# Attention step on TensorE: transposes of the probabilities issued behind the value matmuls of the step instead of ahead of them

## The chip, the cores and the metric

The kernel runs on one core of one Trainium2 chip. The metric is the device time of one launch in microseconds (us). Three runs of the kernel before took 2483.66, 2484.05 and 2486.16 us; the median is 2484.05. A traced execution of it is the source of all profile rows below.

Engines go by the names of the profile: PE is the matrix engine (PEld its weight loads), DVE the vector engine, ACT the scalar engine, POOL the GpSimd engine, SP the engine that issues transfers.

## The reference

Input x is 4 x 1024 tokens of 256 features. One layer in "macaron" form:

```python
x = x + 0.5 * ffn(layernorm(x))       # 8 experts, top 2, and a shared one
x = x + attn(layernorm(x))
x = x + 0.5 * ffn(layernorm(x))
```

The part that matters here is the attention, with 16 heads of 64 features and all 1024 x 1024 scores of each head and batch:

```python
q, k, v = (_ln(x, s, b) @ W + bias for each of q, k, v)
scores = einsum('bhqd,bhkd->bhqk', q, k) / 16
mask = triu(full((S, S), -999.0), k=S - 1)
p = softmax(scores + mask, axis=-1)
att = einsum('bhqk,bhkd->bhqd', p, v)
```

The mask touches one element of each 1024 x 1024 table, the last key of the first query. All of it is in float32. The kernel splits operands into a high and a low part in the matrix engine's reduced float32 format, so that a product is two or three matmuls.

## The kernel before

Four phases follow each other, each written as one function per engine: a feed-forward phase (tiles f_...), the attention (a_...), the output projection and the layer's own MLP (m_...), and the second feed-forward phase (g_...). Engines are kept in step by semaphores that are waited for and counted; the order of instructions on each engine is that of the code.

The attention works in **steps**. A step handles one tile of 128 queries of one head: 64 head-and-batch pairs x 8 tiles = 512 steps. They are grouped in 16 **iterations** of 32 steps (k = 0 to 31; two pairs of heads of one batch), of which 14 run in a hardware loop. Behind them comes a short last part that empties the pipeline. What is computed for one tile is spread over several steps:

- In step k, PE computes the scores of the tile (line 1493, four matmuls of 512 columns into `sc`, which has two buffers). DVE takes the negated row maximum (line 1410), ACT the exponential with its row sum (line 1262, into `pr`).
- In step k + 1, DVE takes the reciprocal of the sum (line 1415) and POOL scales the row (line 1335, `normed`).
- In step k + 3 (`LAG = 3`), PE transposes the 128 x 1024 probabilities with eight transposes in two halves (line 1505, into `tr`, one buffer of two banks, one per half). ACT copies each half to the high part of `pT` (line 1256, `tr_hi`), DVE subtracts it from `tr` and so writes the low part (line 1421, `tr_lo`). `pT` has two buffers, each for four tiles, i.e. 512 queries.
- When four tiles are there they form a **block**. There are 128 of them. The values of a block (line 1529) are 16 matmuls of 512 columns that accumulate in the one bank `ov`. They are cut into four parts of four matmuls, one per step, q = 0 to 3. A block starts (q = 0) in the steps k = 3, 7, 11, ... 31, one step behind the transposes of its last tile. When its last part is done, ACT reads one half of `ov`'s partitions with the bias (line 1249, `ov_read`) and DVE copies the other half (line 1401, `half`). The next block's first matmul waits for both.
- In 12 of the 32 steps PE also computes one piece of the projections of the heads to come (`piece_at`, lines 1448 and 1457, into `pj`): in k = 1, 3, 5, 9, 17, 19, 21, 23, 25, 27, 29 and 31. ACT stages it, POOL splits it.

The order in a step on each engine is this. PE: scores, transposes, values, piece. ACT: read of `ov` if a block has ended in the step before, the two copies of the transposes, the exponential, the staging of the piece. DVE: copy of `ov` if a block has ended, maximum, reciprocal for the step before, the two low parts. POOL: scaling for the step before, the addition of the two head halves at every fourth block, the pieces.

The waits of PE in a step are these: the scores wait for the exponential two steps back (it frees `sc`). The transposes wait for `normed`, and each half of them for the low part of the same half of the tile before (it frees `tr`). At q = 0 the values wait for `tr_lo` of the tile transposed in the step before, for `ov_read` and for `half`:

```python
if q == 0:
    pe.wait_ge(s["tr_lo"], 2 * (u - LAG))
    ...
    if not (first and blk == 0):
        pe.wait_ge(s["ov_read"], it * BLOCKS + blk)
        pe.wait_ge(s["half"], it * BLOCKS + blk)
```

SP moves the second pair's values from a side buffer at the start of each iteration (line 1114), doubles the keys (line 1110), loads weights and stores results.

Of the kernel before, what the change touches and what calls it, by code (L numbers as in the profile page):

```python
# [27 lines left out]
P = 128  # L28
# [916 lines left out]
def attention_phase(nc, turns, tag, w, zT, w_split, bias, att):  # L945
# [14 lines left out]
    LAG = 3  # L960
    QT = S // P
    NP = 4
# [470 lines left out]
    def on_tensor(pe, ahead):  # L1433
# [36 lines left out]
        def body(it, first, last):  # L1470
            for k in steps(last):
                u = it * ITER + k
                slot, head, tile = k // STEPS, (k // QT) % 2, k % QT
                if not last:

                    if k % STEPS == 0:

                        pe.wait_ge(s["k_dup"], it * 64 + slot * 32 + 32)
                        if slot:
                            pe.wait_ge(s["split"], before(it, STEPS))  # L1480
                        elif not first:
                            pe.wait_ge(s["split"], before(it, 0) - 3)
                        else:
                            pe.wait_ge(s["first_split"], 3)
                            pe.wait_ge(f["res"], NB * 2)
                    if first and k == 4:
                        pe.wait_ge(s["first_split"], 4)
                    if not (first and k < 2):

                        pe.wait_ge(s["exp"], u - 1)  # L1490
                    for kb in range(S // BT):
                        for a in range(2):
                            o = pe.matmul(sc[:, k % 2, kb * BT:(kb + 1) * BT],  # L1493
                                          q_s[:, slot, head, tile * P:(tile + 1) * P],
                                          k_s[:, slot, head, a, kb * BT:(kb + 1) * BT],
                                          start=(a == 0), stop=(a == 1))
                    o.then_inc(s["sc"], 1)
                if transposes_at(k, first, last):
                    pe.wait_ge(s["normed"], u - LAG + 1)
                    for part in range(2):  # L1500
                        if not (first and k == LAG):

                            pe.wait_ge(s["tr_lo"], 2 * (u - LAG) + part - 1)
                        for j in range(4):
                            o = pe.transpose(tr[:, part, j * P:(j + 1) * P],  # L1505
                                             pr[:, (k - LAG) % NP, (4 * part + j) * P:(4 * part + j + 1) * P], ident[:])
                        o.then_inc(s["tr"], 1)
                v = values_at(k, first)
                if v and not (last and v[2] >= 0):
                    vslot, vhead, blk, q = v  # L1510
                    if q == 0:

                        pe.wait_ge(s["tr_lo"], 2 * (u - LAG))
                        if blk == 0 and first:
                            pe.wait_ge(s["split"], before(it, 4))
                            pe.wait_ge(f["zT_lo"], (NB + 1) * DC)
                        elif blk == 0:

                            pe.wait_ge(s["split"], before(it, 0))
                        if blk == 4:  # L1520

                            pe.wait_ge(s["v_in"], it * 16 + 16)
# [4 lines that stand above are left out]
                    for kt in (2 * q, 2 * q + 1):  # L1527
                        for a in range(2):
                            o = pe.matmul(ov[:], v_s[:, vslot, kt, 2 * vhead:2 * vhead + 2]  # L1529
                                          .rearrange("p k f -> p (k f)"), pT[:, blk % 2, a, kt],  # L1530
                                          start=(kt == 0 and a == 0), stop=(kt == QT - 1 and a == 1))
                    if q == 3:
                        o.then_inc(s["pv"], 1)
                if not last and piece_at(it, k):
                    kind, part, n, _ = piece_at(it, k)
                    if kind == "K" and part == 0:
                        pe.wait_ge(s["wqk_in"], it * 64 + (k // STEPS) * 32 + 64)
                        if k >= STEPS:
                            pe.wait_ge(s["z_in"], it * 32 + 64)
                    if kind == "V" and part == 0:  # L1540
                        pe.wait_ge(s["wv_in"], it * 16 + 32)
                    project(kind, part, n, False)
                if ends(it) and k == STEPS + 4:
                    ahead["b1"](pj)
                if first and k in (5, 6):
                    if k == 6:
                        pe.wait_ge(f["zT_lo"], NB * DC + 1)
                    rest["zT_up"](k - 5, ov[:])
# [512 lines left out]
```

## Time and profile before

| what | value |
|---|---|
| median of three runs | 2484.05 us |
| profiled execution, its own time | 2480.43 us |
| its span | 2478.6 us |
| PE busy | 2415.1 us, 97% |
| PEld busy | 2097.6 us, 85% |
| DVE busy | 1893.6 us, 76% |
| ACT busy | 1664.7 us, 67% |
| POOL busy | 1505.0 us, 61% |
| granted clock, mean | 0.996 |

The span is what the trace covers, and 1.8 us of the profiled execution's time lie around it. Busy time is that of an engine's instructions; weight loads are counted apart, since they overlap matmuls. The ends of matmuls are modelled, so that a row's duration says less than the distance from its start to the start of the next. A row of the timeline merges neighbouring instructions of the same kind ("x4") and gives in brackets how long the engine had been idle before and who ended that. [...]

### The profile page before, as it was taken

How to read it: one execution, taken by the hardware profiler on the slowest of the kernel's cores; microseconds unless marked ns; L12 is line 12 of the kernel's file. 1: busy time of each engine (PE TensorE's matmuls, PEld its weight loads, DVE VectorE, ACT ScalarE, POOL GpSimd, SP SyncE). 2: the span in 40 equal slices, each digit the busy share in tenths (PEclk: the TensorE clock that was granted, in tenths of full speed). 3: DMA queues.
4: the chain of work that ended last, by engine and by line, in shares of the span. 5: the costliest groups of instructions: out<-in, count | busy, mean ns of one | idle time of the engine just before them, and what ended most of it. 6: DMA issues, size and time to landing. Idle time of an engine off the chain costs nothing.

```text
span 2478.6 us, 46572 instructions
## 1 busy us (share of the span) xinstructions
PE 2415.1 (97%) x14544; PEld 2097.6 (85%) x14544; DVE 1893.6 (76%) x3626; ACT 1664.7 (67%) x2879; POOL 1505.0 (61%) x1525
## 2 busy tenths in 40 slices
PE   7999979999999999999999999999999999989999
PEld 7888868888888888888888888888888879988888
DVE  4777667878888787887878878788887877766665
ACT  2455567878787787877878778787777853433333
POOL 1233277777776878777787777777768754342211
PEclk9999999999999999999999999999999999999999
DMA  3522432213222122321213212132221354431111
GB/s 134 230 102 87 168 99 73 94 43 98 72 76 94 43 85 72 89 94 43 85 60 93 89 47 93 43 97 72 76 94 43 113 178 152 138 104 35 51 51 43
DMA packets 128038, 220.15 MB, mean 89 GB/s; under 512 B 6922, under 2 KB 89764, under 8 KB 119076
## 3 DMA queue, kind: packets, MB, share of 16 engines
q1 hardware_dynamic: 127908, 218.78, 27.4%
q8 instruction: 37, 0.61, 0.1%
q14 instruction: 93, 0.76, 0.1%
HBM read 114.95 MB, written 53.48 MB: 68 GB/s over the span
## 4 chain that ended last, share of the span: by engine, by line
PE 81%; DVE 8%; issue 6%; POOL 2%; ACT 2%; DMA 1%; SPq 0%; DVEq 0%; ACTq 0%; POOLq 0%
PE a_ov L1529 19%; PE a_sc L1493 18%; PE a_tr L1505 18%; PE a_pj L1448 7%; PE a_pj L1457 4%; PE g_acc L856 3%; PE g_hid L819 3%; PE f_hid L819 2%; PE f_acc L856 2%; PE m_proj L1920 1%; PE f_gbc L898 1%; PE m_acc L1957 1%; DVE f_hp L656 1%; PE m_hid L1986 1%; DVE g_hp L656 1%
## 5 line engine op out<-in xcount | busy, mean ns | idle before, releaser
L1410 DVE TENSOR_REDUCE a_nmax<-a_sc 128x1 f32<-128x1024 f32 x512 | 626.6, 1224 | 259.3 <-PE a_sc L1493 251.0
L1335 POOL TENSOR_SCALAR a_pr<-a_pr,a_rden 128x1024 f32<-128x1024 f32 x512 | 578.1, 1130 | 257.5 <-DVE a_rden L1415 186.5
L1256 ACT ACTIVATE a_pT<-a_tr 128x512 fp32r<-128x512 f32 x1024 | 560.1, 596 | 208.7 <-PE a_tr L1505 202.7
L1421 DVE TENSOR_TENSOR a_pT<-a_tr,a_pT 128x512 fp32r<-128x512 f32 x1024 | 649.4, 676 | 17.5 <-ACT a_pT L1256 17.5
L1529 PE MATMUL a_ov<-a_pT,a_v_s 128*128 128x512 f32 x2048 | 600.5, 415 | 3.2 <-DVE a_half L1401 2.0
L1262 ACT ACTIVATE a_pr<-a_sc,a_nmax 128x1024 f32<-128x1024 f32 x512 | 574.0, 1121 | 32.6 <-DVE a_nmax L1410 29.5
L1493 PE MATMUL a_sc<-a_k_s,a_q_s 128*128 128x512 f32 x2048 | 555.5, 393 | 7.8 <-DMA a_k_s<-a_k_s 7.5
L1505 PEld LDWEIGHTS a_tr<-f_ident,a_pr 128*128 128x128 f32 x4096 | 473.8, 140 | 92.2 <-DVE a_pT L1421 18.5
L1505 PE MATMUL a_tr<-f_ident,a_pr 128*128 128x128 f32 x4096 | 537.6, 273 | 9.2 <-DVE a_pT L1421 9.1
L1493 PEld LDWEIGHTS a_sc<-a_k_s,a_q_s 128*128 128x128 f32 x2048 | 381.0, 189 | 89.0 <-DMA a_k_s<-a_k_s 7.7
L1529 PEld LDWEIGHTS a_ov<-a_pT,a_v_s 128*128 128x128 f32 x2048 | 347.5, 189 | 54.4 <-issue 5.0
L1448 PE MATMUL a_pj<-a_z_s,a_wqk_s 128*128 128x512 f32 x756 | 193.5, 391 | 0.6 <-issue 0.6
L1448 PEld LDWEIGHTS a_pj<-a_z_s,a_wqk_s 128*128 128x128 f32 x756 | 141.7, 188 | 32.7 <-issue 1.0
L454 ACT ACTIVATE g_act_out<-g_hid,f_b 128x512 f32<-128x512 f32 x72 | 49.6, 689 | 148.7 <-PE g_hid L819 148.7
L1225 ACT ACTIVATE a_staged<-a_pj,f_bias 128x512 f32<-128x512 f32 x126 | 86.9, 689 | 88.5 <-PE a_pj L1448 66.3
L454 ACT ACTIVATE f_act_out<-f_hid,f_b 128x512 f32<-128x512 f32 x72 | 49.3, 685 | 119.0 <-PE f_hid L819 119.0
L856 PEld LDWEIGHTS f_acc<-f_w2p,f_hp 128*128 128x128 f32 x864 | 112.1, 190 | 9.3 <-DVE f_hp L656 4.5
L856 PEld LDWEIGHTS g_acc<-g_w2p,g_hp 128*128 128x128 f32 x864 | 112.1, 190 | 8.2 <-DVE g_hp L656 2.9
L856 PE MATMUL f_acc<-f_w2p,f_hp 128*128 128x256 f32 x864 | 115.9, 284 | 2.4 <-DVE f_hp L656 1.8
L856 PE MATMUL g_acc<-g_w2p,g_hp 128*128 128x256 f32 x864 | 115.5, 283 | 1.3 <-DVE g_hp L656 0.9
L819 PE MATMUL f_hid<-f_xT,f_w1p 128*128 128x512 f32 x432 | 115.9, 405 | 0.0
L819 PE MATMUL g_hid<-g_xT,g_w1p 128*128 128x512 f32 x432 | 113.1, 397 | 0.0
(207 smaller groups left out, 3281.7 us busy)
## 6 DMA issues: line engine op xcount, KB each, us to landing
a_z_s<-zT SPq DMA_DIRECT2D x32, 1024.0 KB, 7.7
a_k_s<-a_k_s SPq DMA_DIRECT2D x64, 512.0 KB, 5.6
a_wqk_s<-w_split SPq DMA_DIRECT2D x64, 256.0 KB, 3.1
a_v_s<-a_v_b SPq DMA_DIRECT2D x16, 1024.0 KB, 4.6
att<-a_ao SPq DMA_DIRECT2D x32, 512.0 KB, 2.9
m_in<-att SPq DMA_DIRECT2D x16, 1024.0 KB, 6.0
a_wv_s<-w_split SPq DMA_DIRECT2D x17, 512.0 KB, 3.8
zT<-f_zT SPq DMA_DIRECT2D x8, 1024.0 KB, 3.9
```

The lines of the kernel that those rows point to most:

```text
L819: o = pe.matmul(hid[:, (par + e) % 2], w1p[:, a, (c * NE + x) * HID:(c * NE + x + 1) * HID], xT[:, par, c, b], start=(n == 0), stop=(n == 5))
L856: o = pe.matmul(acc[:, t], hp[:, e % 3, a, t * P:(t + 1) * P], w2p[:, b, x * D:(x + 1) * D], start=False, stop=(e == NE - 1 and (a, b) == ...
L1256: act.activation(pT[:, (u // 4) % 2, 0, 4 * part:4 * part + 4, (u % 4) * P:(u % 4 + 1) * P], tr[:, part].rearrange("p (t q) -> p t q", t=4 ...
L1262: act.activation(pr[:, k % NP], sc[:, k % 2], ACT.Exp, bias=nmax[:, k % NP:k % NP + 1], accum_out=den[:, k % NP:k % NP + 1]).then_inc(s["e ...
L1335: pool.tensor_scalar(pr[:, k % NP], pr[:, k % NP], rden[:, k % NP:k % NP + 1], 1.0, ALU.mult, ALU.mult).then_inc(s["normed"], 1)
L1410: dve.tensor_reduce(nmax[:, k % NP:k % NP + 1], sc[:, k % 2], AX.X, ALU.max, negate=True).then_inc(s["negmax"], 1)
L1421: dve.tensor_tensor(to[:, 1], tr[:, part].rearrange("p (t q) -> p t q", t=4), to[:, 0].bitcast(F32), ALU.subtract).then_inc(s["tr_lo"], 1)
L1448: o = pe.matmul(bank[:], wqk_s[:, "QK".index(kind), c, a], z_s[:, c * 2 + b, part], start=(i == 0), stop=(i == 5))
L1457: o = pe.matmul(bank[:, t * 2 * P:(t + 1) * 2 * P], z_s[:, c * 2 + a, part // 2, col:col + P], wv_s[:, c, b], start=(i == 0), stop=(i == 5))
L1493: o = pe.matmul(sc[:, k % 2, kb * BT:(kb + 1) * BT], q_s[:, slot, head, tile * P:(tile + 1) * P], k_s[:, slot, head, a, kb * BT:(kb + 1) * ...
L1505: o = pe.transpose(tr[:, part, j * P:(j + 1) * P], pr[:, (k - LAG) % NP, (4 * part + j) * P:(4 * part + j + 1) * P], ident[:])
L1529: o = pe.matmul(ov[:], v_s[:, vslot, kt, 2 * vhead:2 * vhead + 2] .rearrange("p k f -> p (k f)"), pT[:, blk % 2, a, kt], start=(kt == 0 an ...
```

## The change

The block of code that issues the transposes is moved, within the step on PE, from ahead of the value matmuls to behind them. It stays ahead of the projection piece. Waits and counts are the same. Nothing in the functions of the other engines changes.

```diff
                     o.then_inc(s["sc"], 1)
-                if transposes_at(k, first, last):
-                    pe.wait_ge(s["normed"], u - LAG + 1)
-                    for part in range(2):
-                        if not (first and k == LAG):
-
-                            pe.wait_ge(s["tr_lo"], 2 * (u - LAG) + part - 1)
-                        for j in range(4):
-                            o = pe.transpose(tr[:, part, j * P:(j + 1) * P],
-                                             pr[:, (k - LAG) % NP, (4 * part + j) * P:(4 * part + j + 1) * P], ident[:])
-                        o.then_inc(s["tr"], 1)
                 v = values_at(k, first)
                 if v and not (last and v[2] >= 0):
...
                     if q == 3:
                         o.then_inc(s["pv"], 1)
+                if transposes_at(k, first, last):
+                    pe.wait_ge(s["normed"], u - LAG + 1)
+                    for part in range(2):
+                        if not (first and k == LAG):
+
+                            pe.wait_ge(s["tr_lo"], 2 * (u - LAG) + part - 1)
+                        for j in range(4):
+                            o = pe.transpose(tr[:, part, j * P:(j + 1) * P],
+                                             pr[:, (k - LAG) % NP, (4 * part + j) * P:(4 * part + j + 1) * P], ident[:])
+                        o.then_inc(s["tr"], 1)
                 if not last and piece_at(it, k):
```

The order on PE before, at the turn from one block to the next in a step without a piece: the last part of a block's values (the first row), the next step's scores and transposes, and the first part of the next block's values, with its waits.

```order
L1529 MATMUL a_ov<-a_pT,a_v_s 128x512 x4
L1493 MATMUL a_sc<-a_k_s,a_q_s 128x512 [waits a_exp]
L1493 MATMUL a_sc<-a_k_s,a_q_s 128x512 x3
L1505 MATMUL a_tr<-f_ident,a_pr 128x128 [waits a_tr_lo,a_normed]
L1505 MATMUL a_tr<-f_ident,a_pr 128x128 x3
L1505 MATMUL a_tr<-f_ident,a_pr 128x128 [waits a_tr_lo]
L1505 MATMUL a_tr<-f_ident,a_pr 128x128 x3
L1529 MATMUL a_ov<-a_pT,a_v_s 128x512 [waits a_half,a_ov_read,a_tr_lo]
L1529 MATMUL a_ov<-a_pT,a_v_s 128x512 x3
```

The same place with the change (the values are now line 1519, the transposes line 1531):

```order
L1519 MATMUL a_ov<-a_pT,a_v_s 128x512 x4
L1531 MATMUL a_tr<-f_ident,a_pr 128x128 [waits a_tr_lo,a_normed]
L1531 MATMUL a_tr<-f_ident,a_pr 128x128 x3
L1531 MATMUL a_tr<-f_ident,a_pr 128x128 [waits a_tr_lo]
L1531 MATMUL a_tr<-f_ident,a_pr 128x128 x3
L1493 MATMUL a_sc<-a_k_s,a_q_s 128x512 [waits a_exp]
L1493 MATMUL a_sc<-a_k_s,a_q_s 128x512 x3
L1519 MATMUL a_ov<-a_pT,a_v_s 128x512 [waits a_half,a_ov_read,a_tr_lo]
L1519 MATMUL a_ov<-a_pT,a_v_s 128x512 x3
```

The transposes between the last part of a block and the first part of the next are now those of the earlier step; those of the later step come behind the waiting row.

A step with a projection piece on PE, before, from the transposes on:

```order
L1505 MATMUL a_tr<-f_ident,a_pr 128x128 [waits a_tr_lo,a_normed]
L1505 MATMUL a_tr<-f_ident,a_pr 128x128 x3
L1505 MATMUL a_tr<-f_ident,a_pr 128x128 [waits a_tr_lo]
L1505 MATMUL a_tr<-f_ident,a_pr 128x128 x3
L1529 MATMUL a_ov<-a_pT,a_v_s 128x512 x4
L1448 MATMUL a_pj<-a_z_s,a_wqk_s 128x512 [waits a_staged,a_z_in,a_wqk_in]
L1448 MATMUL a_pj<-a_z_s,a_wqk_s 128x512 x5
```

The same step with the change:

```order
L1519 MATMUL a_ov<-a_pT,a_v_s 128x512 x4
L1531 MATMUL a_tr<-f_ident,a_pr 128x128 [waits a_tr_lo,a_normed]
L1531 MATMUL a_tr<-f_ident,a_pr 128x128 x3
L1531 MATMUL a_tr<-f_ident,a_pr 128x128 [waits a_tr_lo]
L1531 MATMUL a_tr<-f_ident,a_pr 128x128 x3
L1448 MATMUL a_pj<-a_z_s,a_wqk_s 128x512 [waits a_staged,a_z_in,a_wqk_in]
L1448 MATMUL a_pj<-a_z_s,a_wqk_s 128x512 x5
```

The piece stays last in its step; it now follows the transposes directly. DVE, ACT, POOL and SP have the same rows in the same order before and after.

## Rows read from the trace of the kernel before

**Rows 1.** The page: the span, and PE's busy time and share.

```profile
span 2478.6 us, 46572 instructions
...
PE 2415.1 (97%) x14544; PEld 2097.6 (85%) x14544; DVE 1893.6 (76%) x3626; ACT 1664.7 (67%) x2879; POOL 1505.0 (61%) x1525
```

**Rows 2.** The page: the chain that ended last, by engine and by line.

```profile
PE 81%; DVE 8%; issue 6%; POOL 2%; ACT 2%; DMA 1%; SPq 0%; DVEq 0%; ACTq 0%; POOLq 0%
PE a_ov L1529 19%; PE a_sc L1493 18%; PE a_tr L1505 18%; PE a_pj L1448 7%; PE a_pj L1457 4%; PE g_acc L856 3%; PE g_hid L819 3%; PE f_hid L819 2%; PE f_acc L856 2%; PE m_proj L1920 1%; PE f_gbc L898 1%; PE m_acc L1957 1%; DVE f_hp L656 1%; PE m_hid L1986 1%; DVE g_hp L656 1%
```

**Rows 3.** Stretches: length, busy us per engine, granted clock, DMA share, GB/s.

```profile
346.00:2001.00 1655.00, 1647.32 (x9550) 1401.42 (x9551) 1345.59 (x2211) 1317.80 (x2329) 1259.45 (x1285) 1.00 0.25 77
```

**Rows 4.** Timeline of PE, 1198 to 1216 us: start, length, engine, line, tile.

```profile
1198.70 1.54 PE L1448 MATMUL a_pj<-a_z_s,a_wqk_s 128*128 128x512 f32 x6
1200.08 1.07 PE L1493 MATMUL a_sc<-a_k_s,a_q_s 128*128 128x512 f32 x4
...
1211.10 1.08 PE L1493 MATMUL a_sc<-a_k_s,a_q_s 128*128 128x512 f32 x4
1212.01 1.04 PE L1505 MATMUL a_tr<-f_ident,a_pr 128*128 128x128 f32 x8
1212.81 1.17 PE L1529 MATMUL a_ov<-a_pT,a_v_s 128*128 128x512 f32 x4
1213.82 1.08 PE L1493 MATMUL a_sc<-a_k_s,a_q_s 128*128 128x512 f32 x4
1214.74 1.03 PE L1505 MATMUL a_tr<-f_ident,a_pr 128*128 128x128 f32 x8
1215.56 1.17 PE L1529 MATMUL a_ov<-a_pT,a_v_s 128*128 128x512 f32 x4
```

**Rows 5.** Timeline of ACT and then of DVE, 1212 to 1216 us.

```profile
1212.65 1.09 ACT L1256 ACTIVATE a_pT<-a_tr 128x512 fp32r<-128x512 f32 x2 [0.53 <-PE a_tr L1505]
1213.62 1.12 ACT L1262 ACTIVATE a_pr<-a_sc,a_nmax 128x1024 f32<-128x1024 f32 x1
...
1214.71 0.68 ACT L1249 ACTIVATE a_ao<-a_ov,f_bias 64x512 f32<-64x512 f32 x1
...
1212.21 1.22 DVE L1410 TENSOR_REDUCE a_nmax<-a_sc 128x1 f32<-128x1024 f32 x1 [0.23 <-PE a_sc L1493]
...
1213.42 1.27 DVE L1421 TENSOR_TENSOR a_pT<-a_tr,a_pT 128x512 fp32r<-128x512 f32 x2
1214.72 0.69 DVE L1401 COPY a_half<-a_ov 64x512 f32<-64x512 f32 x1
```

**Rows 6.** The instructions of line 1401: count, ns of one, first and last start.

```profile
L1401 DVE COPY a_half<-a_ov x128: 683/688/694, 358.9 to 2014.7; 64x512 f32<-64x512 f32 x128
```

**Rows 7.** Timeline of PE, ACT and DVE at the attention's end, 2005 to 2015 us.

```profile
2005.05 1.16 PE L1505 MATMUL a_tr<-f_ident,a_pr 128*128 128x128 f32 x8 [0.73 <-DVE a_pT L1421]
...
2009.14 5.50 PE L1529 MATMUL a_ov<-a_pT,a_v_s 128*128 128x512 f32 x16 [2.00 <-DVE a_half L1401]
...
2014.47 0.40 PE L1920 MATMUL m_proj<-m_wo,m_att_hi 128*128 128x256 f32 x2
...
2006.35 1.10 ACT L1256 ACTIVATE a_pT<-a_tr 128x512 fp32r<-128x512 f32 x2
...
2006.99 1.29 DVE L1421 TENSOR_TENSOR a_pT<-a_tr,a_pT 128x512 fp32r<-128x512 f32 x2 [1.49 <-ACT a_pT L1256]
2008.31 0.68 DVE L1401 COPY a_half<-a_ov 64x512 f32<-64x512 f32 x1
```

**Rows 8.** Timeline of SP: the value move of the second and of the fifteenth iteration.

```profile
452.61 0.51 SPq L1114 DMA_DIRECT2D a_v_s<-a_v_b  x1
...
1822.45 0.52 SPq L1114 DMA_DIRECT2D a_v_s<-a_v_b  x1
```

**Rows 9.** Stretches (columns as in rows 3) with the granted clock.

```profile
330.00:346.00 16.00, 11.01 (x62) 7.90 (x62) 11.66 (x24) 13.24 (x26) 12.10 (x18) 1.00 0.36 127
...
2010.00:2012.00 2.00, 2.00 (x6) 1.61 (x5) 2.00 (x2) 0.00 (x0) 0.00 (x0) 0.50 0.00 0
```

## The prediction, made before the change was run

> **What bounds the kernel now.** I read the page's busy shares first. PE is busy 97% of the 2478.6 us span [rows 1], and the chain of waits gives PE 81% of it, more than half of the span to three lines of the attention step: 1529 (values, ov), 1493 (scores, sc) and 1505 (transposes, tr) [rows 2]. The table of stretches then says where: from 346 to 2001 us PE is busy 1647 of 1655 us at full clock, DVE 1346, ACT 1318, POOL 1259 [rows 3]. So attention is bound by PE's own instructions, and anything that makes PE stand still there goes into the time in full.
>
> The timeline of PE gives a step's pace, start to start: sc to tr 0.91 (1211.10 to 1212.01), tr to ov 0.80, ov to sc 1.01 [rows 4], together 2.72 us. A projection piece adds 1.38 (pj to sc) [rows 4]. An iteration of the loop has 32 steps and 12 pieces, so 32 x 2.72 + 12 x 1.38 = 103.6 us if PE never waits. The trace has 13 iterations between two issues of the value move, 1822.45 - 452.61 = 1369.8 us, 105.4 each [rows 8]. PE thus waits only 1.8 us per iteration now, some 29 us over the 16.
>
> What matters is why PE hardly waits at the turn of a block. The values of one block take four steps (q = 0 to 3) and accumulate in the one PSUM bank ov. At q = 0 PE must wait until the last block's ov was read by ACT (line 1249) and DVE (line 1401), and until the transposes of the step before are copied (tr_lo). The trace shows such a turn: ACT's read runs from 1214.71 to 1215.39, DVE's copy from 1214.72 to 1215.41 [rows 5], and ov starts at 1215.56 [rows 4]. That ov came only 0.82 after the transposes ahead of it instead of 0.80. The reads started at 1214.71, just as PE went into the new step's transposes (1214.74), and these 0.8 us of transposes are exactly what covers them.
>
> **The change, part by part.** Nothing is added or removed: PE has the same instructions with the same waits, and DVE, ACT, POOL and SP the same work in the same order. PE's order in a step becomes sc, ov, tr, piece.
>
> 1. Pace without waits. Before, the handovers in a step were 512 columns to 128 (sc to tr), 128 to 512 (tr to ov), 512 to 512 (ov to sc or pj). After, they are 512 to 512 (sc to ov), 512 to 128 (ov to tr), 128 to 512 (tr to sc or pj): the same kinds once each. I take zero. As a bound, a group of four 512-column matmuls takes 0.91 or 1.01 depending on its neighbours [rows 4]; if one group of each step changed between these, 512 steps would give 51 us either way.
>
> 2. The turn of a block. Call T the start of the last transposes ahead of the turn (step q = 3). Until now PE ran tr, then ov (q = 3), sc and tr of the next step, then ov (q = 0): from T that is 0.80 + 1.01 + 0.91 + 0.80 = 3.52 us of work. Now it runs only tr and sc: T + 0.80 + 1.01 = T + 1.81. (I take tr to sc as the 0.80 of tr to ov and sc to ov as the 1.01 of ov to sc.) What must be done by then stands in fixed order on the two other engines:
> ACT: first half of pT 0.64 after the transposes start (1212.01 to 1212.65), the exponential 0.97 later (1213.62), the read of ov 1.09 later (1214.71), 0.68 long [rows 4, 5], and 0.17 from its end (1215.39) to ov's start (1215.56). Sum 0.64 + 0.97 + 1.09 + 0.68 + 0.17 = 3.55 us.
> DVE: pT's low part 0.64 after ACT's first copy starts (2006.35 to 2006.99), 1.32 to the copy of ov (2008.31), 0.68 long, and 0.15 to ov [rows 7]; with the same 0.64 ahead that is 3.43.
> That 3.55 just meets 3.52 is why the turn costs nothing today. In the new order ov stands at T + 1.81 and has to wait until T + 3.55: 1.74 us of standstill, and behind the waiting ov all of PE's queue stands too, this step's transposes, the piece and the next scores. None of the work can fill the gap: no piece lies in a step with q = 3 (pieces are at 1, 3, 5, 9, 17, 19, 21, 23, 25, 27, 29, 31; q = 3 at 2, 6, 10, and so on). Is the exponential late for another reason? It needs the maximum of its step. The transposes of the step before start at T - 2.72, so DVE ends their low part at T - 2.72 + 0.64 + 0.64 + 1.30 = T - 0.14, and the maximum (1.21 from start to the next work [rows 5]) at T + 1.07, while ACT comes to the exponential at T + 1.61. So no. Nor does DVE become the bound: 4 x (1.21 + 1.30) + 0.7 = 10.7 us in a block that will last 4 x 2.72 + 1.74 = 12.6.
> There are 128 blocks [rows 6]. One has no block before it and the last turn lies behind the last scores, where the trace already shows this very wait (2.00 us idle, put down to the copy of ov [rows 7]); it stays. That leaves 126 turns: 126 x 1.74 = 219 us.
>
> 3. Waits that go. The 29 us worked out above are waits of the transposes for DVE and small ones at turns. In the new order the transposes come 1.0 later than the scores, so DVE has that much longer, and the turn's gap takes in the rest. I let them all go: -29. The bound on the other side is 0.
>
> 4. Last iteration and DMA. Without scores and with three transposes left, the order is set by waits on DVE's copies both times: zero. Key, query, weight loads and the att stores hang on pieces and blocks, which all come later together: zero.
>
> Sum: 219 - 29 = +190 us. The profiled execution took 2480.4 and would become 2670; the median of the runs is 2484.05, 3.6 above it, and would be **2674 us**.
>
> [...]
> [...]
>
> **The rivals.**
> A. The clock falls at the turns. For it: the tail. Price: the 16 value matmuls behind the standstill took 2009.14 to 2014.47 = 5.33 us [rows 7] where four groups at 1.01 are 4.04, so 1.3 us each, 126 x 1.3 = 164: 2838 us. Against it: the 330 to 346 stretch. 5%.
> B. Faster: the turn stays hidden and only point 3 remains. This is decided at the moment when ACT and DVE take up the old ov: if by T + 1.81 less 0.17 both reads were over, PE would not wait, and 29 us would be saved: 2455 us. The reads wait for the last ov matmul, which now ends ahead of the transposes, about 1 us earlier, and that speaks for it. Against it: in each engine's order the read stands behind the exponential and behind pT's low part of these transposes, so that it can't start before T + 2.7. 2%.
> C. The reads do come early, but ov (q = 0) still waits for the low parts of the transposes issued just ahead: 0.64 + 0.64 + 1.30 + 0.15 = 2.73 after T, a wait of 0.92, 126 x 0.92 - 29 = +87: 2571 us. Same argument against it as for B. 3%.
> D. No change, because waits elsewhere on PE or between engines just move: PE's 97% leaves nothing into which 1.7 us per block could move. 2%.
> The forecast with its bounds has 88%.
>
> **How the numbers follow.** Ends of the forecast: with DVE's chain (3.43) as the one that counts, 126 x 1.62 = 204, less 29, +175: 2659; with some of point 1's bound in PE's favour (20 of its 51 us) 2639. With no waits given back, +219: 2703; with 20 us of point 1 against it, 2723. So **2639 to 2723**. It holds about 84%; A, B, C and D lie outside. A measurement of this kernel tells a difference from none from about 0.2% on. Faster by more than that only in B (0.02), within it in D (0.02), slower in the forecast, A and C (0.96).
>
> **What would show it right or wrong.** Right: PE idle ahead of the value matmuls, 127 or so times, 1.6 to 1.8 us each, some 220 us, released by the ov read of ACT (line 1249) or the copy of DVE (1401); the value move every 105.4 + 8 x 1.74 - 1.8 = 117.5 us; PE's busy time unchanged near 2415 us with a share of about 90%; no more waits of the transposes for pT; granted clock 1.00 in the loop. Wrong: a clock below 1.00 in the loop (A); no wait at the turns (B); the wait ended by pT's low part, under 1 us (C); a step without a turn that lasts longer or shorter than 2.72 (point 1).

## The result, and the profile after

| | before | after |
|---|---|---|
| median of 4 runs | 2485.11 us | 2712.14 us (2708.79 to 2716.69) |
| ratio | | 1.0917, 95% interval 1.0902 to 1.0932 |
| profiled execution, its span | 2478.6 us | 2710.0 us |
| granted clock, mean, as a share of full speed | 0.996 | 0.986 |

The change costs 227 us between the medians and 231.4 us between the two spans. Forecast were +190 us, 2674 us, and 2639 to 2723 us as the range: the direction and the mechanism came true, the size came out 37 us short.

The page of the kernel after, the lines that answer to [rows 1, 2]:

```profile
span 2710.0 us, 46684 instructions
...
PE 2453.0 (91%) x14544; PEld 2108.9 (78%) x14544; DVE 1931.2 (71%) x3626; ACT 1636.9 (60%) x2879; POOL 1504.4 (56%) x1525
...
PE 71%; ACT 11%; issue 8%; DVE 7%; POOL 2%; DMA 1%; ACTq 1%; SPq 0%; DVEq 0%; POOLq 0%
```

PE's share fell from 97 to 91%, and in the chain of waits ACT, which had 2%, now has 11%. PE's busy time went up by 38 us, with the same 14544 matmuls, where the prediction had it unchanged; part of it lies in the stretches at a granted clock of 0.50 shown below, in which the same matmuls take longer (eight transposes 1.42 us instead of 0.79).

The list of waits on PE, from 346 to 2230 us (engine, line, releaser, us in total, times, longest):

```profile
PE a_ov L1519 <- ACT a_ao L1249: 198.1, 126, 2.0
```

There were 126 turns in the prediction, and the trace has this wait 126 times, 1.46 to 2.0 us each. The waits of the transposes for pT's low part, 18.5 us on the weight loads before, are gone. (The idle time is a little less than the delay itself, in the turn below 1.46 us against 3.43 - 1.81 = 1.62, since the modelled end of the matmul ahead reaches into the gap.)

A turn in a block without a piece, on PE, ACT and DVE (start, length, engine, line, tile). It is the place that answers to [rows 4, 5]:

```profile
1209.32 1.04 PE L1531 MATMUL a_tr<-f_ident,a_pr 128*128 128x128 f32 x8
1210.12 1.17 PE L1493 MATMUL a_sc<-a_k_s,a_q_s 128*128 128x512 f32 x4
1212.75 1.20 PE L1519 MATMUL a_ov<-a_pT,a_v_s 128*128 128x512 f32 x4 [1.46 <-ACT a_ao L1249]
1213.79 1.03 PE L1531 MATMUL a_tr<-f_ident,a_pr 128*128 128x128 f32 x8
...
1209.96 1.09 ACT L1256 ACTIVATE a_pT<-a_tr 128x512 fp32r<-128x512 f32 x2 [0.53 <-PE a_tr L1531]
1210.93 1.12 ACT L1262 ACTIVATE a_pr<-a_sc,a_nmax 128x1024 f32<-128x1024 f32 x1
...
1212.02 0.68 ACT L1249 ACTIVATE a_ao<-a_ov,f_bias 64x512 f32<-64x512 f32 x1
...
1210.59 1.29 DVE L1421 TENSOR_TENSOR a_pT<-a_tr,a_pT 128x512 fp32r<-128x512 f32 x2 [0.22 <-ACT a_pT L1256]
1211.91 0.69 DVE L1401 COPY a_half<-a_ov 64x512 f32<-64x512 f32 x1
```

With T = 1209.32 the reader finds each member of the predicted sum: ACT's copies at T + 0.64, the exponential at T + 1.61, the read at T + 2.70 until T + 3.38, ov at T + 3.43 (predicted 3.55; the last handover took 0.05 us, not 0.17). DVE's copy ends at T + 3.28. The scores of the step start at T + 0.80, and without a wait ov would have followed at T + 1.81. Behind the wait, ov to tr takes 1.04 us and not 0.91.

Not all turns are alike. Those at k = 11, 15, 27 and 31 have PE idle for 1.46 to 1.47 us, whether the block has projection pieces or not. Those at k = 3, 19 and 23 are dearer by 0.15 us. In these ACT's read starts 1.23 us after the exponential instead of 1.09; the block that has ended is one of the second head of its pair each time. Why the read then comes later was not looked into. The first row below is the first kind (k = 27), the others are a turn of the second (k = 3):

```profile
1257.77 1.20 PE L1519 MATMUL a_ov<-a_pT,a_v_s 128*128 128x512 f32 x4 [1.46 <-ACT a_ao L1249]
...
1285.27 1.03 PE L1531 MATMUL a_tr<-f_ident,a_pr 128*128 128x128 f32 x8
1286.06 1.17 PE L1493 MATMUL a_sc<-a_k_s,a_q_s 128*128 128x512 f32 x4
1288.84 1.19 PE L1519 MATMUL a_ov<-a_pT,a_v_s 128*128 128x512 f32 x4 [1.62 <-ACT a_ao L1249]
...
1286.88 1.12 ACT L1262 ACTIVATE a_pr<-a_sc,a_nmax 128x1024 f32<-128x1024 f32 x1
...
1288.11 0.68 ACT L1249 ACTIVATE a_ao<-a_ov,f_bias 64x512 f32<-64x512 f32 x1
```

One turn of each iteration is the longest, that at k = 7, the first behind the value move of SP: ACT's read has the same late start, and another 0.2 us pass between the read's end (1184.33) and ov (1184.58), for which the trace gives no reason. The clock falls to 0.50 behind this turn in 11 of the 15 iterations from 464 us on. PE, then the stretches around it (columns as in [rows 3]):

```profile
1180.81 1.03 PE L1531 MATMUL a_tr<-f_ident,a_pr 128*128 128x128 f32 x8
1181.60 1.17 PE L1493 MATMUL a_sc<-a_k_s,a_q_s 128*128 128x512 f32 x4
1184.58 1.16 PE L1519 MATMUL a_ov<-a_pT,a_v_s 128*128 128x512 f32 x4 [1.82 <-ACT a_ao L1249]
1185.58 1.77 PE L1531 MATMUL a_tr<-f_ident,a_pr 128*128 128x128 f32 x8
1187.00 2.06 PE L1493 MATMUL a_sc<-a_k_s,a_q_s 128*128 128x512 f32 x4
...
1184.00:1186.00 2.00, 1.42 (x7) 1.23 (x8) 1.37 (x3) 0.33 (x1) 1.94 (x2) 0.93 0.43 168
1186.00:1188.00 2.00, 2.00 (x9) 1.81 (x8) 0.69 (x1) 1.20 (x2) 1.71 (x3) 0.50 0.00 0
```

Eight transposes take 1.42 us here to the next scores instead of 0.79, and the scores 1.86 to ov (at 1188.86) instead of 1.01. Taken in stretches of 2 us from 366 to 2225 us, the clock is below 1.00 behind this turn in 11 iterations and nowhere else; the kernel before has no such stretch between 346 and 2001 us. One more fall, at 346 us, stands behind the wait of the first block's values (2.09 us idle).

In the other four of the loop's iterations the turn at k = 7 is just as long, and the turns ahead of it are too, but the clock stays at 1.00:

```profile
708.01 1.16 PE L1519 MATMUL a_ov<-a_pT,a_v_s 128*128 128x512 f32 x4 [1.82 <-ACT a_ao L1249]
```

What a fall costs can be read from the value moves of SP, one per iteration, that answer to [rows 8]:

```profile
464.50 0.51 SPq L1114 DMA_DIRECT2D a_v_s<-a_v_b  x1
584.45 0.52 SPq L1114 DMA_DIRECT2D a_v_s<-a_v_b  x1
704.43 0.52 SPq L1114 DMA_DIRECT2D a_v_s<-a_v_b  x1
822.76 0.52 SPq L1114 DMA_DIRECT2D a_v_s<-a_v_b  x1
...
2137.36 0.52 SPq L1114 DMA_DIRECT2D a_v_s<-a_v_b  x1
```

Iterations last 119.95 us with a fall (464.50 to 584.45) and 118.33 without (704.43 to 822.76): 1.6 us each. Of the 14 intervals 10 are long and 4 short, mean 119.5, against 105.4 before.

The attention's end, as in [rows 7]:

```profile
2230.18 1.16 PE L1531 MATMUL a_tr<-f_ident,a_pr 128*128 128x128 f32 x8 [0.74 <-DVE a_pT L1421]
2234.27 6.78 PE L1519 MATMUL a_ov<-a_pT,a_v_s 128*128 128x512 f32 x16 [2.92 <-DVE a_half L1401]
2240.88 0.40 PE L1920 MATMUL m_proj<-m_wo,m_att_hi 128*128 128x256 f32 x2
```

Transposes to values are 4.09 us, to the hundredth what they were. But PE now stands idle for 2.92 us instead of 2.00, as the last ov part lies ahead of the transposes, and the sixteen matmuls take 6.61 us, 5.33 before: the granted clock is 0.50 from 2234 to 2240 us, and before it was 0.50 from 2010 to 2012 and 0.70 in the 2 us behind.

### The profile page after: what moved, and what is told of

It reads as the page before. It is cut to its first block, busy times and chain, and to the rows that moved or that the text cites. A ratio compares the mean times of both kernels' runs of the same rounds, so it can differ in the third digit from the quotient of the medians.

```text
span 2710.0 us, 46684 instructions
## 1 busy us (share of the span) xinstructions
PE 2453.0 (91%) x14544; PEld 2108.9 (78%) x14544; DVE 1931.2 (71%) x3626; ACT 1636.9 (60%) x2879; POOL 1504.4 (56%) x1525
## 4 chain that ended last, share of the span: by engine, by line
PE 71%; ACT 11%; issue 8%; DVE 7%; POOL 2%; DMA 1%; ACTq 1%; SPq 0%; DVEq 0%; POOLq 0%
PE a_ov L1519 19%; PE a_tr L1531 15%; PE a_sc L1493 13%; PE a_pj L1448 6%; ACT a_pr L1262 5%; PE a_pj L1457 3%; ACT a_ao L1249 3%; PE g_acc L856 2%; PE g_hid L819 2%; PE f_acc L856 2%; PE f_hid L819 2%; ACT a_pT L1256 1%; PE m_proj L1920 1%; PE m_acc L1957 1%; PE f_gbc L898 1%
## 5 line engine op out<-in xcount | busy, mean ns | idle before, releaser
L1421 DVE TENSOR_TENSOR a_pT<-a_tr,a_pT 128x512 fp32r<-128x512 f32 x1024 | 660.4, 686 | 337.2 <-ACT a_pT L1256 336.4
L1519 PE MATMUL a_ov<-a_pT,a_v_s 128*128 128x512 f32 x2048 | 572.9, 402 | 203.1 <-ACT a_ao L1249 198.1
L1519 PEld LDWEIGHTS a_ov<-a_pT,a_v_s 128*128 128x128 f32 x2048 | 378.3, 190 | 333.6 <-ACT a_ao L1249 192.7
L1493 PE MATMUL a_sc<-a_k_s,a_q_s 128*128 128x512 f32 x2048 | 589.9, 410 | 7.8 <-DMA a_k_s<-a_k_s 7.4
L1531 PEld LDWEIGHTS a_tr<-f_ident,a_pr 128*128 128x128 f32 x4096 | 485.9, 142 | 75.1 <-issue 6.0
L1493 PEld LDWEIGHTS a_sc<-a_k_s,a_q_s 128*128 128x128 f32 x2048 | 361.8, 192 | 62.5 <-DMA a_k_s<-a_k_s 7.7
L1448 PE MATMUL a_pj<-a_z_s,a_wqk_s 128*128 128x512 f32 x756 | 205.3, 407 | 0.0
L1448 PEld LDWEIGHTS a_pj<-a_z_s,a_wqk_s 128*128 128x128 f32 x756 | 133.4, 190 | 21.9
L454 ACT ACTIVATE f_act_out<-f_hid,f_b 128x512 f32<-128x512 f32 x72 | 49.3, 684 | 118.3 <-PE f_hid L819 118.3
L819 PE MATMUL g_hid<-g_xT,g_w1p 128*128 128x512 f32 x432 | 113.1, 397 | 0.0
L1457 PE MATMUL a_pj<-a_wv_s,a_z_s 128*128 128x256 f32 x768 | 108.4, 291 | 0.4 <-ACT a_staged L1225 0.4
```

What stands on the lines that cost most here:

```text
L819: o = pe.matmul(hid[:, (par + e) % 2], w1p[:, a, (c * NE + x) * HID:(c * NE + x + 1) * HID], xT[:, par, c, b], start=(n == 0), stop=(n == 5))
L1421: dve.tensor_tensor(to[:, 1], tr[:, part].rearrange("p (t q) -> p t q", t=4), to[:, 0].bitcast(F32), ALU.subtract).then_inc(s["tr_lo"], 1)
L1448: o = pe.matmul(bank[:], wqk_s[:, "QK".index(kind), c, a], z_s[:, c * 2 + b, part], start=(i == 0), stop=(i == 5))
L1457: o = pe.matmul(bank[:, t * 2 * P:(t + 1) * 2 * P], z_s[:, c * 2 + a, part // 2, col:col + P], wv_s[:, c, b], start=(i == 0), stop=(i == 5))
L1493: o = pe.matmul(sc[:, k % 2, kb * BT:(kb + 1) * BT], q_s[:, slot, head, tile * P:(tile + 1) * P], k_s[:, slot, head, a, kb * BT:(kb + 1) * ...
L1531: o = pe.transpose(tr[:, part, j * P:(j + 1) * P], pr[:, (k - LAG) % NP, (4 * part + j) * P:(4 * part + j + 1) * P], ident[:])
```

## The experiments

Eleven kernels, each timed beside the kernel before on the same chip. "Loop" is the distance between two value moves, without a fall of the clock where both occur.

| run | median us | ratio to before | loop us |
|---|---|---|---|
| the change | 2712.1 | 1.092 | 118.3 |
| 1: old order in k = 2, 3 | 2675.3 | 1.077 | 116.5 |
| 2: ACT reads early | 2675.4 | 1.076 | 117.2 |
| 3: ACT and DVE read early | 2610.6 | 1.050 | 113.1 |
| 4: old order at q = 0 | 2579.0 | 1.038 | 111.3 |
| 5: old order at q = 3 and 0 | 2480.3 | 0.997 | 104.8 |
| 6: values a step later | 2670.8 | 1.076 | 116.1 |
| 7: the same, both reads early | 2468.3 | 0.992 | 104.0 |
| 8: as 5, old order in k = 12, 13 too | 2475.6 | 0.996 | 104.5 |
| 9: old order at q = 3 | 2592.5 | 1.044 | 111.9 |
| 10: as 6, ACT alone early | 2630.4 | 1.059 | 113.4 |
| 11: old order in k = 6, 7 | 2664.0 | 1.073 | 116.5 |

### Where the cost sits: the order put back step by step

Runs 1, 4, 5, 8, 9 and 11 issue the transposes ahead of the values in some steps only. The block of code stands twice in the step, under two conditions:

```diff
+    def ahead_at(k):
+        return (k - LAG - 4) % 4 == 0
...
+                if transposes_at(k, first, last) and ahead_at(k):
+                    ...
                 v = values_at(k, first)
...
-                if transposes_at(k, first, last):
+                if transposes_at(k, first, last) and not ahead_at(k):
```

**Run 4**, the steps with q = 0 (the condition shown).

> The changed kernel, with the transposes ahead of the values again in the steps with q = 0 alone. Theory: the reads still come at T + 3.55, T being the start of the transposes of q = 3 behind the block's last values, but PE has those of the step q = 0 to do meanwhile (0.8 us), so each turn costs 1.0 us in place of 1.8: 2712 - 126 x 0.8 = 2611 us less the clock's 18 us, about 2595 us. Rival (the moved transposes cost time in every step, not at the turn): three steps of four are still changed, so three quarters of the 227 us stay: 2655 us.

Measured: 2578.97 us, ratio 1.0382 (1.0365 to 1.0399), 16 us under the expectation. Three steps of four still have the new order, and 133 of the 227 us are gone, so most of the cost sits at the turn. The wait for the read of ov shrank to 33 us in all. The 0.8 us of work put back at the turn took 7.0 us off the loop's 118.3, 0.88 per turn.

**Run 9**, the steps with q = 3 (condition `== 3`).

> The changed kernel, with the transposes ahead of the values again in the steps with q = 3 alone. Theory: from the transposes of q = 3 PE now has tr 0.80, ov 1.01, sc 0.92 and reaches the next block's values at T + 2.7, where the reads are over at T + 3.5: 0.8 us at each of 126 turns is 100 us on top of the 2480 us of the run with both steps in the old order: 2560 to 2590 us, within 20 us of the run with q = 0 alone. Rival (which of the two neighbours of the turn has the old order does not matter by its work but by position): far from it on either side.

Measured: 2592.45 us, ratio 1.0442 (1.0426 to 1.0459), 13 us from run 4 and 2 us above the range expected. A turn of it, on PE, ACT and DVE:

```profile
1210.54 1.04 PE L1508 MATMUL a_tr<-f_ident,a_pr 128*128 128x128 f32 x8
...
1213.24 0.67 ACT L1252 ACTIVATE a_ao<-a_ov,f_bias 64x512 f32<-64x512 f32 x1
1213.26 0.69 DVE L1404 COPY a_half<-a_ov 64x512 f32<-64x512 f32 x1
...
1214.10 1.17 PE L1532 MATMUL a_ov<-a_pT,a_v_s 128*128 128x512 f32 x4 [0.67 <-DVE a_half L1404]
```

From the last transposes to ov it is 3.56 us, where the change has 3.43. ACT's read starts at T + 2.70 as there; DVE's copy starts at T + 2.72, 0.13 us later than there, and ends this wait (of 124 waits of ov, 63 are put down to DVE and 61 to ACT). So the readers are nearly where they were, and what differs is what PE has to do meanwhile.

**Run 5**, both (condition `in (3, 0)`).

> The changed kernel, with the transposes ahead of the values again in the steps with q = 3 and q = 0, on both sides of the turn; only the steps with q = 1 and 2 stay changed. Theory: the turn has its cover back and costs nothing. What stays is the change of order from q = 2 to q = 3: the transposes of q = 3 come 1 us sooner behind those of q = 2 and wait for the low parts of pT, about 0.6 us each time as in the run with q = 0 alone. So 2484 - 29 + 126 x 0.6 = 2531 us. Rival (every moved step costs): half of the 227 us, 2598 us. If the order inside q = 1 and 2 and the change over cost nothing at all: 2455 us.

Measured: 2480.28 us, ratio 0.9970 (0.9957 to 0.9984). With the old order on both sides of the turn nothing of the loss is left, and the half of the steps that stay changed cost nothing. But the 0.6 us for the change of order from q = 2 to q = 3 was wrong in seven blocks of eight. The eighth shows it, on PE:

```profile
577.75 1.04 PE L1544 MATMUL a_tr<-f_ident,a_pr 128*128 128x128 f32 x8
578.54 1.17 PE L1496 MATMUL a_sc<-a_k_s,a_q_s 128*128 128x512 f32 x4
579.76 1.25 PE L1508 MATMUL a_tr<-f_ident,a_pr 128*128 128x128 f32 x8
580.78 1.17 PE L1532 MATMUL a_ov<-a_pT,a_v_s 128*128 128x512 f32 x4
581.79 1.08 PE L1496 MATMUL a_sc<-a_k_s,a_q_s 128*128 128x512 f32 x4
```

This is k = 14, behind k = 13, the one step with q = 2 and no piece: from its scores to the next ones it takes 3.25 us, 0.53 above the pace. In all other blocks a piece of 1.4 us lies between the two groups of transposes, and no such delay is seen there.

**Run 8** puts that block right (condition `in (3, 0) or k in (12, 13)`).

> As the run with the old order at q = 3 and 0, and the old order also in the steps k = 12 and 13, so that the one block without a projection piece at q = 2 has no change of order. Theory: a change from sc, ov, tr to sc, tr, ov costs 0.53 us where no piece lies between the two groups of transposes, and nothing where one does (k = 13 is the only step with q = 2 and no piece). 16 x 0.53 = 8 us less, minus 2 to 4 us of the kernel before's own waits in that block: 2472 to 2476 us. Rival (the 0.53 us are the order's own price, or noise of one place): no change, 2480 us.

Measured: 2475.61 us, ratio 0.9963 (0.9949 to 0.9977). Between the medians of runs 5 and 8 that is 4.7 us, but the kernel before, timed beside each, differs by 3.2 us as well. The better evidence is the loop, which fell from 104.83 to 104.52, 0.31 x 16 = 5 us. So the place was named rightly and its 0.53 us came back less what the old order waits there itself.

**Run 1**, one turn of each iteration (condition `k in (2, 3)`), meant for the longest one, behind which the clock fell.

> The changed kernel, with the transposes ahead of the values again in the steps k = 2 and 3 alone, which is the first turn of each iteration (one of eight). Theory: this turn's wait goes, and with it the fall of the clock that follows that turn in most iterations (about 1.6 us each, as an iteration with it lasts 119.95 us and one without 118.32). Against that the transposes of step 2 come 1 us sooner behind those of step 1 and wait some 0.6 us for the low part of pT. So about 1.85 - 0.6 = 1.2 us x 16 plus 11 x 1.6 are saved: 2712 - 19 - 18 = 2675 us, all iterations alike at 116.5 to 117.2 us, clock 1.00 in the loop. Rival (the falls are brought on by the eight gaps together, not by this longer one): 2693 us, with falls as before.

Measured: 2675.27 us, ratio 1.0765 (1.0746 to 1.0784). The total met the number, but by errors that cancelled. The turn brought back its whole 1.8 us (the loop went from 118.3 to 116.5), not 1.2, since a piece lies in k = 1 and covers the change of order. And k = 3 was the wrong turn: the value move is issued when the values of step k = 6 are done, so the long turn behind it is that of k = 7. It was still there, and still had a fall behind it in 4 of 14 intervals, each 1.6 us longer than the others, where the change had 10. The gap at k = 7 was at least 1.81 us long in every iteration, with a fall and without. So the run could not say whether the long gap brings on the falls, but it says that its length alone does not.

**Run 11** takes the right one (condition `k in (6, 7)`).

> The changed kernel, with the old order in the steps k = 6 and 7 alone. This is the turn behind which the value move is issued, the longest of the eight (2.98 us from scores to values, the others 2.63 to 2.79), and the one behind which the clock fell; run 1, meant for it, had taken the ordinary turn at k = 3 away. Theory: the long gap brings on the falls. With it gone they all go, every loop iteration lasts 118.3 - 2.0 = 116.3 us, the clock is 1.00 in the loop: 2712 - 32 - 18 = 2662 us, some 13 us less than with the turn at k = 3 gone. Rival (the falls hang on the sum of the gaps or on chance, as their drop from 10 to 4 of 14 in run 1 suggests): falls at other turns, 2665 to 2680 us, with some iterations 1.6 us longer than others.

Measured: 2664.01 us, ratio 1.0726 (1.0711 to 1.0741), as the theory has it. The 14 intervals lie between 116.43 and 116.54 us, and no stretch of 2 us in the loop's iterations is below 1.00 from the value move at 466 us on. (Ahead of the loop there is one fall, at 405 us, and it stands behind a gap of 1.81 us too.) Against run 1, with as many turns covered, 11 us are saved, part of it the falls. So the falls in the changed kernel's loop hang on its longer gap, PE idle for 1.81 us or more. What else decides is open. In run 1 the turn at k = 3 was gone, but the iteration was shorter as well, so that every gap came at another moment; the two were not told apart.

### What the chain consists of: the reads of ov moved on ACT and DVE

**Run 2**: ACT reads ov in the step in which the block ends, between its copies and the exponential.

```diff
+    def ended_at(k, first, last):
+        v = values_at(k, first)
+        return v if v and v[3] == 3 and not (last and v[2] >= 0) else None
...
-                v = finished_at(k, first)
-                if v:
-                    vslot, vhead, blk, _ = v
...
                 if transposes_at(k, first, last):
...
+                v = ended_at(k, first, last)
+                if v:
+                    vslot, vhead, blk, _ = v
...
                 if not last:
                     u = it * ITER + k
                     act.wait_ge(s["negmax"], u + 1)
```

> The changed kernel, with ACT's read of ov one step earlier in its order, ahead of the exponential of the step in which the block ends. Theory: ACT's chain is then 0.64 + 0.97 + 0.68 = 2.3 us from the last transposes and no longer decides; DVE's chain (3.4 us) decides, so little is won: 0.1 us in plain blocks, up to 0.3 in those with pieces, 126 x 0.1 to 0.3 = 13 to 35 us, about 2690 us, with the waits now put down to DVE's copy (line 1401 before). Rival (ACT's order alone makes the wait): ov could start at T + 2.5, 126 x 1 us less, 2586 us.

Measured: 2675.37 us, ratio 1.0761 (1.0740 to 1.0782). The rival's 2586 us is out. The loop lost 1.1 us, 0.14 per turn, and no stretch below full clock was left in it, which is worth another 18 us that the expectation had not counted. The list of waits now names DVE, as the theory has it:

```profile
PE a_ov L1524 <- DVE a_half L1406: 172.2, 118, 1.5
```

**Run 3**: DVE's copy is moved in the same manner, to between the maximum and the reciprocal.

> As the run before, and DVE's copy of ov too is taken one step earlier, between the maximum and the low parts of pT of the step in which the block ends. Theory: both reads are over at T + 2.3, but the values of the next block also need the low parts of the transposes just issued, which now stand behind the copy on DVE: ov starts at about T + 3.3. So 2680 to 2690 us, with pT's low part as what ends the wait. Rival (only the reads of ov hold PE up): ov at T + 2.4, about 2712 - 126 x 1.1 = 2573 us or less.

Measured: 2610.59 us, ratio 1.0503 (1.0485 to 1.0520). The wait is now put down to pT's low part, as the theory has it, but the time lies 70 us under what it gave. A turn in a block with pieces, and the waits:

```profile
1207.10 1.03 PE L1536 MATMUL a_tr<-f_ident,a_pr 128*128 128x128 f32 x8
...
1207.64 0.69 DVE L1415 COPY a_half<-a_ov 64x512 f32<-64x512 f32 x1
...
1208.43 1.29 DVE L1426 TENSOR_TENSOR a_pT<-a_tr,a_pT 128x512 fp32r<-128x512 f32 x2
...
1209.97 1.17 PE L1524 MATMUL a_ov<-a_pT,a_v_s 128*128 128x512 f32 x4 [0.91 <-DVE a_pT L1426]
...
PE a_ov L1524 <- DVE a_pT L1426: 116.0, 123, 1.4
```

From T = 1207.10 ov comes at T + 2.87, not 3.3. I had taken DVE's times from a plain block, where the maximum ends at T + 1.1 and the copy delays the low parts. Such a turn is still there at k = 15: PE is idle for 1.37 us and ov starts at T + 3.3. In blocks with pieces DVE has caught up; its copy starts at T + 0.54 and the low parts at T + 1.33, hardly later than without it. This wait of the values is a third member of the chain: it is what rival C of the prediction named, only hidden behind the reads.

**Run 6**: the values of each block lie one step later, so that they no longer need the transposes issued just ahead.

```diff
-        return range(LAG + 5 if last else ITER)
+        return range(LAG + 6 if last else ITER)
...
-        j = k - LAG - 4
+        j = k - LAG - 5
...
-                        pe.wait_ge(s["tr_lo"], 2 * (u - LAG))
+                        pe.wait_ge(s["tr_lo"], 2 * (u - LAG - 1))
```

> The changed kernel, with the values of every block one step later, so that they no longer need the low parts of the transposes issued just ahead, while the reads of ov stay where they are in the orders of ACT and DVE. Theory: the reads alone decide, and they lie as far behind the last transposes ahead of the turn as before, so nothing is won: 2695 to 2715 us, the lower end if the clock no longer falls. Rival (the low parts are what holds PE up): 2600 us or less.

Measured: 2670.76 us, ratio 1.0755 (1.0719 to 1.0790). The rival is out, since ACT's read still ends the wait (149 us in 119 waits) and a plain turn lasts 4.46 us from scores to scores as in the change. The time lies 24 us or more under the expectation, because I had not seen that the move puts the piece of five steps (k = 3, 19, 23, 27, 31) into the gap. Four of those turns last 0.7 to 1 us less; the fifth, now at k = 0, lasts 1.2 us longer than a plain one. PE is idle for 2.7 to 2.9 us there, and the clock fell at or behind this gap in 7 of the 14 intervals and behind the turn of 1.81 us in one more.

**Run 10**: as run 6, with ACT's read ahead of its copies, DVE's copy left.

> The values one step later and ACT's read early, but DVE's copy of ov left behind the low parts. Theory: DVE's chain (3.4 us from T, of which PE's own work covers 1.8, and 3.2 where a piece lies in the step) decides: three turns of eight wait 1.6 us, five 0.2 to 0.3 us, so 16 x 6 = 95 us more than the run with both reads early: about 2560 us. Rival (ACT's read alone was what held PE up): 2468 to 2480 us.

Measured, in two executions only: 2630.38 us, ratio 1.0589 (1.0564 to 1.0615). The rival is far out: ACT alone is not what held PE up. The size was missed by 70 us. The early read delays ACT's copies and with them DVE, so that the values start 3.77 us after the transposes where a piece lies in the step. In 6 of the 14 intervals there is a fall of the clock besides, behind gaps of 1.83 to 1.91 us. A turn:

```profile
1212.15 1.04 PE L1536 MATMUL a_tr<-f_ident,a_pr 128*128 128x128 f32 x8
1212.56 0.69 ACT L1254 ACTIVATE a_ao<-a_ov,f_bias 64x512 f32<-64x512 f32 x1 [0.30 <-PE a_ov L1524]
...
1215.08 0.69 DVE L1406 COPY a_half<-a_ov 64x512 f32<-64x512 f32 x1
...
1215.92 1.16 PE L1524 MATMUL a_ov<-a_pT,a_v_s 128*128 128x512 f32 x4 [0.37 <-DVE a_half L1406]
```

**Run 7**: as run 6, with both reads early (DVE's as in run 3, ACT's ahead of its copies).

> As the run before, and ACT reads ov ahead of its copies of the step in which the block ends, DVE copies it between the maximum and the low parts. Theory: ACT is done 0.9 us behind T, DVE between 1.3 and 1.9 us, PE comes at 1.8 us and waits 0.15 us at most in plain blocks; no low part is in the way. The moved order then costs nothing and the waits that the kernel before has in its transposes are gone: 2455 to 2480 us, faster than the kernel before by up to 29 us. Rival (the order sc, ov, tr has a price of its own, or DVE, with 10.8 us of work in a plain block of 10.9, becomes the bound): 2490 to 2520 us.

Measured: 2468.25 us, ratio 0.9923 (0.9910 to 0.9937). This is the fastest kernel of the study, 0.8% under the kernel before, with the transposes behind the values in every step. All three members of the chain are off the turn, and the loop lasts 104.0 us, within 0.4 us of the 103.6 that the prediction worked out for a PE that never waits. A turn of it, the same place in the program as the first one shown:

```profile
1206.33 1.04 PE L1536 MATMUL a_tr<-f_ident,a_pr 128*128 128x128 f32 x8
1206.62 0.68 ACT L1254 ACTIVATE a_ao<-a_ov,f_bias 64x512 f32<-64x512 f32 x1 [0.19 <-PE a_ov L1524]
1207.12 1.17 PE L1498 MATMUL a_sc<-a_k_s,a_q_s 128*128 128x512 f32 x4
...
1207.33 0.69 DVE L1415 COPY a_half<-a_ov 64x512 f32<-64x512 f32 x1
...
1208.17 1.15 PE L1524 MATMUL a_ov<-a_pT,a_v_s 128*128 128x512 f32 x4
```

ACT's read starts 0.29 us behind T, DVE's copy 1.00 us, and ov follows at T + 1.84. It could be so late only because the values come a step later, and they can come a step later only with the new order (or with more waits): transposes ahead of the values would overwrite a pT buffer that the last part of the block two before still reads (this is read from the code and was not tried).

## Why the prediction was right, and what it missed

**What bounds the kernel**: right. A standstill of PE went into the time in full.

**Point 1, the pace without waits**: right at zero. Steps without a turn last 2.72 us, or 2.61 and 4.18 in pairs where there were 2.72 and 4.08: the sum of a pair is the same within 0.01 us. Runs 5 and 7 confirm it with half of the steps and with all of them in the new order.

**Point 2, the turn**: the mechanism is shown. The wait appears in the trace at each of the 126 turns and goes when PE's cover is put back (run 5) or the reads are moved away (run 7). At four of the eight turns its size was as predicted: 1.74, measured 4.46 - 2.72 = 1.74 between the scores of that step (1210.12) and the next (1214.58). That it is exact is luck: two small errors cancel there, 0.12 us less of a chain and 0.13 us more from ov to tr behind the wait. At three turns it is 0.15 us more and at k = 7 it is 0.35, of which the sum had nothing. Over the eight turns the loop lost 118.3 - 103.6 = 14.7 us, 1.84 per turn and not 1.74, and a value move comes every 118.3 us without a fall where 117.5 were forecast. Over 16 iterations that is 13 of the missing us.

**Point 3, the waits that go**: the waits of the transposes went. Of the 29 us no separate part can be told apart from the turns in the changed kernel; run 7 shows that they can be had, with 105.4 - 104.0 = 1.4 us of the 1.8 per iteration.

**Point 4**: the order of the last part cost nothing in itself (4.09 us both times), but its sixteen matmuls, at 0.50 for most of their time, were 1.3 us dearer (6.61 and 5.33 us).

**The clock is the term that was missed.** Two stretches of the kernel before bore on it [rows 9]: 0.50 from 2010 to 2012 us, right behind the 2.00 us idle of [rows 7], the tail that rival A goes by, and 1.00 from 330 to 346 us, where PE was busy for only 11.0 of 16 us. The forecast went by the second and priced the clock at zero. But that stretch holds no idle time as long as the one at k = 7; its longest is 1.48 us (kernel before, PE):

```profile
332.71 1.16 PE L1505 MATMUL a_tr<-f_ident,a_pr 128*128 128x128 f32 x8 [1.48 <-DVE a_pT L1421]
```

The clock fell behind one turn of the eight, and there in 11 iterations of the traced execution, for 11 x 1.6 = 18 us. Run 11 shows that without this turn's gap it does not fall in the loop; the four iterations without a fall show that the gap by itself is not enough. Rival A had the mechanism and the price per fall nearly right (1.3 predicted, 1.6 measured); the mistake lay in taking all turns as alike, so that it was either none or all 126. The turn at k = 7 is longer than the others: PE is idle for 1.82 us there, against 1.46 and 1.62 at the others.

The sum then is 190 + 13 + 18 = 221 of the 231 us between the spans. Of the remaining 10, 1.3 are those of the sixteen last matmuls, and 4.9 lie in the phases that the change does not touch: from the first matmul of the output projection (2240.88, and 2014.47 before) to the end of the span it is 469.1 us, and 464.2 before. The clock falls three times there between 2420 and 2450 us where the kernel before has one fall. But the kernels of all eleven runs take 467.3 to 472.5 us for the same phases, also those of runs 5, 7 and 8 (467.3, 470.1 and 470.5 us), which are no slower than the kernel before. So these 4.9 us are likely no part of the change; with one trace of the kernel before this is not shown. The last 4 us, in the attention, were not settled.

**Rivals B, C and D** are refuted as they stand. For B and C the reads would have had to come early, and they could not. The low parts of C exist as a limit (run 3), 2.9 us behind T where C had 2.73. D put the change at nothing, and it cost 227 us.

## What to carry to other kernels

Before moving work past a wait, ask what that work covers. Here the readers of the one bank stand in line on other engines behind work that a group of transposes feeds, and are done about 3.4 us after it starts. In the old order PE had 3.5 us of its own work from those transposes to the reuse of the bank; in the new one it has 1.8. An order that looks neutral in PE's instruction count can be put right, or turned into a gain, by moving the readers: first find every member of the chain, since taking one away (run 2: 0.14 us per turn) only shows the next.

## What the runs showed of the hardware

In the change the granted clock dropped to 0.50 (1186 to 1188 us, for one) in a loop that keeps PE busy for nine tenths of the time (1497.5 of 1672.9 us from 464.5 us on). With eight gaps of 1.5 to 1.8 us idle in an iteration of 118 us it fell in 10 of 14, always behind the longest gap, and each fall cost 1.6 us. With that gap gone (run 11) or shortened to 1.5 us (run 2) it held in every loop iteration; with an ordinary gap gone, the one ahead of it, it fell in 4 of 14 (run 1).

Taken over all kernels here, every fall in a loop iteration stands at or behind a gap of 1.8 us or more (the change and runs 1, 6 and 10); none stands behind one of 1.7 us or less, of which run 10 has one of 1.69 in each iteration. But a gap of 1.8 us or more can be without one: the 1.8 us had none behind them in 4 iterations of the change (1.81 and 1.82 us idle), and in run 6 even 2.7 us had none in 6. What decides there was not found, so it can't be said in which iterations a fall will come.

A stretch of 16 us with PE busy for 11 of them had kept a clock of 1.00 [rows 9], so PE's share alone does not tell; its longest gap was 1.48 us.
